# Another order for the last steps of the cross attention and the routing

## The chip, the cores and the metric

The kernel is one program on one core of a Trainium2 chip. Its time is the device time of one execution in microseconds (us), taken over several executions. A separate profiled execution leaves the trace from which the rows below come. Engines are named as the profile names them: PE is the matrix engine, DVE the vector engine, ACT the scalar engine, POOL the engine that scatters rows, SP the queue that issues the plain transfers.

## What is computed

The reference is one decoder layer on 8 sequences of 112 tokens and 512 features (896 tokens, 7 tiles of 128), in fp32:

```python
x = _layernorm(x + _L0_attn_ref(x, W_Q, W_K, W_V, W_O))              # 16 heads, causal
x = _layernorm(x + _L0_xattn_ref(x, ctx_2048, Wq, Wg, bg, Wkv, Wo))  # 375 context rows per sequence
x = _layernorm(x + _L0_ffn_ref(x, router_weight, router_bias, ...))  # 8 experts, the best 2 of each token

# _L0_xattn_ref, cut
kv_summary = jnp.einsum('bhsd,bhse->bhde', k, v)    # k, q through a feature map
z = 1.0 / (jnp.einsum('bhld,bhd->bhl', q, k_sum)[..., None] + EPS)
attn = jnp.einsum('bhld,bhde->bhle', q, kv_summary) * z
out = attn * gate @ Wo.T

# _L0_ffn_ref, cut
logits = h @ router_weight.T + router_bias
top_vals, top_idx = jax.lax.top_k(logits, TOP_K)
...
expert_out = jnp.einsum('eti,eih->eth', act, down_proj) + down_proj_bias[:, None, :]
out = jnp.einsum('te,eth->th', scores, expert_out)
```

## The kernel before

Every engine runs a list of steps that is written out by hand, and waits on semaphores. Large products are split in two parts of the operands and take three passes, so a 128x512 result over 512 features is 12 matmuls (helper `products`, L275). The program goes through the causal attention (two heads at a time), then the linear cross attention, then the routing and the eight experts.

The place of the change is the end of the cross attention and the whole of the late routing. The context of a sequence b is three chunks of 125 rows, so there are 24 chunks n. On PE a chunk is `ctx_k(n)` and `ctx_v(n)`, 12 matmuls each, and `sums(n)`, which adds it to the summary of its sequence in banks 4 and 5. `sums_out(b)` on DVE (L1329) moves the finished summary out, and `attended(b)` on PE (L659) multiplies the queries of sequence b with it. DVE's `attended(b)` divides, `turn_atn(b)` on PE (L668) transposes, and `gated(b)` on DVE (L1393), `a_high(b)` on ACT and `a_low(b)` on DVE make the two parts of the product's input. `cross_out(n)` on PE (12 matmuls, L275 with w_xo) is the output product of token tile n; tile n needs the sequences that it touches, and tiles 5 and 6 need sequences up to 6 and 7.

A token tile then goes through a chain. `cross_add(n)` on DVE adds and takes the statistics, POOL's `inverse_std` makes the inverse deviation, `x2_norm(n)` on DVE (L1350) writes the normalised `row`. `turn_x2(n)` on PE (L686) transposes it, `x2_copy(n)` on ACT (L1026) takes it out of its bank, `router(n)` on PE (L693) makes 8 logits, and `choose(n)` on DVE picks two experts (`chosen`, L1435). `rank(n)` on PE (L703, L704) counts the places in the experts' lists, `assign(n)` on DVE makes the slots (`slot_u`, L1462), and `scatter(n)` on POOL (L425) sends the rows to the experts' lists in HBM. After the last scatter SP fetches the rows of the first three experts (`rows_in`, L352).

Beside it `turn_score(n)` and `down_bias(n)` on PE (L716, L723) make the sum of the experts' output biases of a tile, with `score_copy(n)` on ACT between them; `bias_add(n)` on DVE (L1467) adds it to the row, and `base_store(n)` on SP (L333) writes that to the accumulator in HBM.

The lists are in `block` functions, one for each engine. `CHUNKS` says which chunks run in which iteration of a loop over sequences: four, four, four, three and two; chunk 23 comes behind the loop. Which of the eight PSUM banks a result takes is the place of its step in `late_order` (banks 0 to 3) or `route_order` (banks 6 and 7 by turns); PE waits until the bank's last use has been read. PE enters the expert stage by `gather(0, k)` (L854), the transposes of the fetched rows in banks 4 and 5, and then `gate_up_part` for expert 0 (L275 with w_gu).

Of the kernel before, what the change touches and what calls it, by code (L numbers as in the profile page):

```python
# [23 lines left out]
def decoder_layer(nc: bass.Bass, t: dict, out: bass.AP):  # L24
# [17 lines left out]
    CHUNKS = ((6, 7, 8, 9), (10, 11, 12, 13), (14, 15, 16, 17), (18, 19, 20), (21, 22))  # L42
    DUMP = 3 * P

    with ExitStack() as ctx:
# [175 lines left out]
        def late_order():  # L221
# [13 lines left out]
            rest += [("num", 10), ("num", 11), ("ck", 23), ("turn", 5), ("cv", 23), ("num", 12), ("num", 13), ("wo", 4),  # L235
                     ("turn", 6), ("wo", 5), ("num", 14), ("num", 15), ("turn", 7), ("wo", 6)]
# [3 lines left out]
        def route_order():  # L240
            steps = []
            for n in range(4):
                steps += [("t1", n), ("rt", n), ("rk", n)]
            steps += [("st", 0), ("db", 0), ("t1", 4), ("st", 1), ("db", 1), ("rt", 4), ("t1", 5), ("rt", 5), ("rk", 4),
                      ("rk", 5), ("t1", 6), ("st", 2), ("db", 2), ("rt", 6), ("st", 3), ("db", 3), ("rk", 6), ("cnt", 0)]
            for n in range(4, NT):
                steps += [("st", n), ("db", n)]
            for i, (what, n) in enumerate(steps):
                yield what, n, 6 + i % 2

# [32 lines left out]
        def _(sp):  # L283
# [62 lines left out]
            base_store(0)  # L346
            base_store(1)
# [14 lines left out]
            for n in range(2, NT):  # L362
                base_store(n)
# [41 lines left out]
        def _(pool):  # L405
# [25 lines left out]
            for n in range(4):  # L431
# [62 lines left out]
        def _(pe):  # L494
            late, route = late_order(), route_order()

            def take(of, what, n):
                assert next(of)[:2] == (what, n), (what, n)
                k, turn = place[what, n]
                if turn > 1:  # L500
                    pe.wait_ge(free[k], turn - 1)
                return banks[k]
# [311 lines left out]
            router(3)  # L814
            attended(5)
            sums(22)
            rank(3)
            ctx_k(23)
            turn_atn(5)
            ctx_v(23)  # L820
            attended(6)
            cross_out(4)
            turn_atn(6)
# [12 lines left out]
            rank(4)  # L836
            cross_out(6)
            rank(5)
            turn_x2(6)
            turn_score(2)  # L840
            down_bias(2)
            router(6)
            turn_score(3)
            down_bias(3)
            rank(6)
            count()
            for n in range(4, NT):
                turn_score(n)
                down_bias(n)
# [47 lines left out]
            for k in range(4):  # L897
# [37 lines left out]
        def _(act):  # L935
# [172 lines left out]
            top_tanh(3)  # L1108
# [12 lines left out]
            feature_k(23)  # L1121
            a_high(5)
            score_copy(0)
            a_high(6)
            x2_copy(4)
            score_copy(1)
            top_tanh(4)
            a_high(7)
            x2_copy(5)
            gu_high(0, 0, 0)  # L1130
            top_tanh(5)
            gu_high(0, 0, 1)
            score_copy(2)
            x2_copy(6)
            score_copy(3)
            top_tanh(6)
            gu_high(0, 0, 2)
            gu_high(0, 0, 3)
            for n in range(4, NT):
# [83 lines left out]
        def _(dve):  # L1223
# [386 lines left out]
            choose(3)  # L1610
            attended(5)
            assign(3)
            phi(23)
            gated(5)
            a_low(5)
            v_copy(23)
            attended(6)
            cross_add(4)
            gated(6)
            a_low(6)  # L1620
            sums_out(7)
            x2_norm(4)
            cross_add(5)
            attended(7)
            bias_add(0)
# [175 lines left out]
```

## Time and profile before

| what | us |
|---|---|
| median of 3 runs | 939.78 |
| lowest and highest | 939.7, 941.78 |
| the profiled execution's own time | 941.92 |
| its span, first to last instruction | 940.1 |
| PE busy in the span | 851.5 |
| DVE, ACT, POOL busy | 468.1, 307.7, 100.5 |

All times below are counted from the start of the span. The cross attention's loop runs up to about 640, the routing's last steps from there to 707, and the first expert's products start at 711.04. A row of the timeline gives start, duration, engine, line, operation, result and operands, count, and in square brackets the idle time before it with what ended it. Starts of neighbouring PE rows are up to 0.3 us closer than their durations say, since matmuls overlap and their ends are modelled.

### The profile page before, as it was taken

To read this page: it belongs to the slowest core of one execution; us is meant where nothing else is said; L and a number is where in the kernel's file an instruction comes from. 1 tells how busy PE (TensorE), PEld (TensorE's weight loads), DVE (VectorE), ACT (ScalarE), POOL (GpSimd) and SP (SyncE) were. 2 spreads that over 40 slices of the span, in tenths; PEclk is the share of its full clock that TensorE was granted. 3 is DMA by queue.
4 is the path that set the end of the run, shared out by engine and by line. 5 is a ranking of instruction groups with operands and counts; after the bars stand their busy time and mean duration, and the time that the engine had idled before them with its cause. 6 is when DMAs were issued, how large, how long until landed. Compare 5 with 4: busy or idle time off the path is not lost.

```text
span 940.1 us, 12579 instructions
## 1 busy us (share of the span) xinstructions
PE 851.5 (91%) x4967; PEld 745.8 (79%) x4967; DVE 468.1 (50%) x853; ACT 307.7 (33%) x666; POOL 100.5 (11%) x95
## 2 busy tenths in 40 slices
PE   6999999999999999699999999989769699999990
PEld 5998999999898989578898777778538687877760
DVE  3435454544545352838622443444553666666634
ACT  4443333332314132422442211121212444455430
POOL 0000000000000000000000010101021133333343
PEclk9999999999999999989999999999757799999995
DMA  9940817250202020013100111102455266655225
GB/s 324 353 140 1 260 45 237 69 180 1 90 1 90 1 101 12 1 45 124 33 1 1 33 45 45 56 23 69 156 182 144 107 185 185 185 160 160 70 32 178
DMA packets 34461, 96.99 MB, mean 103 GB/s; under 512 B 5720, under 2 KB 7768, under 8 KB 31712
## 3 DMA queue, kind: packets, MB, share of 16 engines
q1 hardware_dynamic: 30592, 87.70, 27.2%
q0 software_dynamic: 3808, 8.46, 4.6%
q8 instruction: 41, 0.67, 0.3%
q14 instruction: 20, 0.16, 0.1%
HBM read 64.03 MB, written 32.12 MB: 102 GB/s over the span
## 4 chain that ended last, share of the span: by engine, by line
PE 79%; DVE 9%; ACT 5%; issue 5%; DMA 1%; SPq 0%; POOLq 0%; POOL 0%; DVEq 0%; ACTq 0%
PE bank L275 65%; PE bank L589 3%; PE bank L536 2%; PE bank L621 2%; ACT w_gu L937 2%; PE bank L579 1%; PE bank L723 1%; ACT x_g L1145 1%; DVE prob L1263 1%; DVE hh L1687 1%; PE bank L693 1%; PE bank L512 1%; DVE ln_st L1339 1%; DVE up L1678 1%; PE bank L659 1%
## 5 line engine op out<-in xcount | busy, mean ns | idle before, releaser
L275 PE MATMUL bank<-w_kv,cT 128*125 128x512 f32 x576 | 147.5, 407 | 6.5 <-DVE cT L1225 6.5
L275 PE MATMUL bank<-xT,w_qkv 128*128 128x448 f32 x672 | 137.7, 365 | 0.0
L275 PEld LDWEIGHTS bank<-xT,w_qkv 128*128 128x128 f32 x672 | 126.1, 188 | 10.6 <-ACT qT L958 0.4
L275 PEld LDWEIGHTS bank<-w_kv,cT 128*125 128x125 f32 x576 | 106.4, 190 | 31.2 <-DVE cT L1225 6.9
L275 PE MATMUL bank<-x_g,w_gu 128*128 128x288 f32 x768 | 111.0, 303 | 10.1 <-DVE w_gu L1225 9.3
L275 PEld LDWEIGHTS bank<-x_g,w_gu 128*128 128x128 f32 x768 | 107.2, 194 | 11.2 <-DVE w_gu L1225 9.4
L275 PE MATMUL bank<-w_qkv,xT 128*112 128x256 f32 x672 | 85.3, 283 | 0.0
L275 PE MATMUL bank<-w_dn,hT 128*128 128x512 f32 (+1 forms) x288 | 69.9, 397 | 12.4 <-ACT y L1164 10.3
L275 PE MATMUL bank<-w_o,zT 128*128 128x512 f32 x336 | 79.6, 394 | 0.5 <-DVE acc L1540 0.5
L275 PEld LDWEIGHTS bank<-w_qkv,xT 128*112 128x112 f32 x672 | 79.9, 175 | 0.0
L415 POOL TENSOR_TENSOR ln_rs<-ln_ve,half 128x1 f32<-128x1 f32 (+2 forms) x16 | 12.7, 794 | 593.8 <-DVE ln_ve L1345 593.8
L275 PEld LDWEIGHTS bank<-w_o,zT 128*128 128x128 f32 x336 | 61.8, 188 | 14.8 <-DVE acc L1252 1.8
L275 PEld LDWEIGHTS bank<-w_dn,hT 128*128 128x128 f32 (+1 forms) x288 | 45.4, 161 | 33.7 <-ACT y L1164 12.9
L1225 DVE TENSOR_TENSOR w_qkv<-raw_w,w_qkv 128x1024 fp32r<-128x1024 f32 x21 | 25.7, 1225 | 62.4 <-ACT w_qkv L937 62.4
L967 ACT ACTIVATE prob<-prob,neg_max 112x112 f32<-112x112 f32 x128 | 47.7, 374 | 24.3 <-DVE neg_max L1267 24.3
L994 ACT ACTIVATE relu_c<-bank 125x512 f32<-125x512 f32 x24 | 14.3, 598 | 125.1 <-PE bank L275 125.1
L977 ACT CAST zT<-bank 128x448 fp32r<-128x448 f32 x32 | 17.1, 533 | 98.9 <-PE bank L589 98.9
L1311 DVE SCALAR_TENSOR_TENSOR phi_k<-exp_c,relu_c 125x512 f32<-125x512 f32 x24 | 16.6, 692 | 63.4 <-ACT exp_c L995 63.4
L1241 DVE COPY V<-bank 112x512 f32<-112x512 f32 x32 | 22.1, 692 | 51.2 <-PE bank L275 51.2
L463 POOL DMA_INDIRECT y_acc<-y,meta x24 | 41.4, 1724 | 50.0 <-ACT y L1164 45.9
L1252 DVE TENSOR_TENSOR acc<-acc,bank 128x512 f32<-128x512 f32 x49 | 33.6, 687 | 26.1 <-PE bank L275 26.1
L1225 DVE TENSOR_TENSOR w_gu<-raw_gu,w_gu 128x1024 fp32r<-128x1024 f32 x32 | 39.0, 1225 | 8.5 <-ACT w_gu L937 8.5
(144 smaller groups left out, 1169.3 us busy)
## 6 DMA issues: line engine op xcount, KB each, us to landing
x_rows<-blank SPq DMA_DIRECT2D x9, 2084.0 KB, 19.3
raw_gu<-in_w_gu_dram SPq DMA_DIRECT2D x8, 2048.0 KB, 7.8
raw_w<-in_w_qkv_dram SPq DMA_DIRECT2D x21, 512.0 KB, 6.8
raw_dn<-in_w_down_dram SPq DMA_DIRECT2D x8, 1024.0 KB, 8.3
raw_c<-in_ctx_t_dram SPq DMA_DIRECT2D x8, 750.0 KB, 4.4
raw_o<-in_w_o_dram SPq DMA_DIRECT2D x8, 512.0 KB, 3.7
xg<-x_rows SPq DMA_DIRECT2D x8, 512.0 KB, 6.9
raw_kv<-in_w_kv_dram SPq DMA_DIRECT2D x2, 1024.0 KB, 7.0
```

The lines of the kernel that those rows point to most:

```text
L275: last = nc.tensor.matmul(mm_out, lhs(a, k), rhs(b, k), start=(k == 0 and i == 0), stop=(k == n - 1 and i == 2))
L463: nc.gpsimd.indirect_dma_start(y_acc, bass.IndirectOffsetOnAxis(ap=number(k, rows).bitcast(U32), axis=0), y[0:rows, slot(k), :], None, bou ...
L536: mm = nc.tensor.matmul(banks[j][:, 0:HALF], w_first[:, part, a, k, h * E:(h + 1) * E], xT[:, b, k, hf * HALF:(hf + 1) * HALF], start=(k = ...
L589: mm = nc.tensor.matmul(banks[6 + g % 2][:, j * S:(j + 1) * S], V[0:S, p % 2, hf * BH + j, h * E:(h + 1) * E], probT[0:S, g % 2, j, :], st ...
L621: mm = nc.tensor.matmul(banks[4 + g // 2][:, (g % 2) * G1:(g % 2 + 1) * G1], phi_k[0:CM, n % 3, g * P:(g + 1) * P], v_c[0:CM, n % 3, g, :] ...
L937: return nc.scalar.copy(dst, src)
L967: e = nc.scalar.activation(prob[0:S, g, j, :], prob[0:S, g, j, :], ACT.Exp, bias=neg_max[0:S, i:i + 1], scale=-1.0, accum_out=exp_sum[0:S, ...
L977: nc.scalar.copy(zT[:, 0, h, hf * HALF:(hf + 1) * HALF], banks[6 + g % 2][:, 0:HALF])\
L1225: return nc.vector.tensor_tensor(dst, src, bits(hi), ALU.subtract)
L1241: nc.vector.tensor_copy(V[0:S, p % 2, 2 * j:2 * j + 2, :], banks[(1 + j) % 2][0:S, :].rearrange("p (a c) -> p a c", a=2))\
L1252: nc.vector.tensor_tensor(acc[:, n, :], acc[:, n, :], banks[n % 2][:, :], ALU.add)\
L1311: nc.vector.scalar_tensor_tensor(phi_k[0:CM, n % 3, :], exp_c[0:CM, n % 2, :], 1.0, relu_c[0:CM, n % 2, :], ALU.min, ALU.add).then_inc(m[" ...
```

## The change

It is an order change; every engine executes the same computation as before.

- The last three chunks 21, 22 and 23 go one to each of the iterations of sequences 4, 5 and 6, and the token tile's steps are one iteration later than in the loop before.
- The eighth sequence's steps (attended, turn_atn, gated) and cross_out(5), cross_out(6) come ahead of the routing steps of tiles 5 and 6. turn_x2 and router of both tiles stand together, ahead of rank(5) and of the score transposes.
- From turn_score(0) on, the routing's results go round banks 6, 4, 5, 7. The first use of 4 or 5 waits until the summaries have left them (`sum_out`).
- Only bias product 0 stays ahead of rank(6); 1 to 6 stand behind it. PE's gather waits for banks 0 to 5 ahead of its first transpose.
- POOL takes inverse_std(4) ahead of scatter(3), and inverse_std(6) ahead of scatter(4).
- SP issues all seven base stores behind the fetch of the rows; two of them stood ahead of the second expert's weights.

```diff
-    CHUNKS = ((6, 7, 8, 9), (10, 11, 12, 13), (14, 15, 16, 17), (18, 19, 20), (21, 22))
+    CHUNKS = ((6, 7, 8, 9), (10, 11, 12, 13), (14, 15, 16, 17), (18, 19, 20))
...
             for i, (what, n) in enumerate(steps):
                 yield what, n, 6 + i % 2
+            last = [("st", 0), ("rk", 4), ("db", 0), ("t1", 5), ("rt", 5), ("t1", 6), ("rt", 6),
+                     ("rk", 5), ("st", 1), ("rk", 6), ("cnt", 0), ("db", 1)]
+            for n in range(2, NT):
+                last += [("st", n), ("db", n)]
+            for i, (what, n) in enumerate(last):
+                yield what, n, (6, 4, 5, 7)[i % 4]
...
             sp.dma_start(raw_dn[1], t["w_down"][1]).then_inc(in_dn[1], 16)
-            base_store(0)
-            base_store(1)
             sp.wait_ge(*ready("wo", NT - 1))
...
-            for n in range(2, NT):
+            for n in range(NT):
                 base_store(n)
...
-            for n in range(4):
+            for n in range(3):
                 inverse_std(1, n, n + 1, n + 3)
                 scatter(n)
+            inverse_std(1, 3, 4, 6)
             inverse_std(1, 4, 5, 7)
+            scatter(3)
             inverse_std(1, 5, 6, 8)
+            inverse_std(1, 6, 7, 9)
             scatter(4)
-            inverse_std(1, 6, 7, 9)
             scatter(5)
             scatter(6)
...
+                elif k in (4, 5):
+                    pe.wait_ge(m["sum_out"], 2 * NB)
...
+            for b in range(4, 7):
+                n = b + 17
+                attended(b)
+                sums(n - 1)
+                ctx_k(n)
+                turn_atn(b)
+                if b > 4:
+                    turn_x2(b - 2)
+                ctx_v(n)
+                if b > 4:
+                    router(b - 2)
+                if b < 6:
+                    cross_out(b - 1)
+                if b == 5:
+                    rank(3)
             sums(23)
             turn_score(0)
+            attended(7)
             cross_out(5)
-            attended(7)
+            turn_atn(7)
+            rank(4)
             down_bias(0)
-            turn_x2(4)
-            turn_score(1)
-            down_bias(1)
-            router(4)
-            turn_atn(7)
+            cross_out(6)
             turn_x2(5)
             router(5)
-            rank(4)
-            cross_out(6)
+            turn_x2(6)
+            router(6)
             rank(5)
-            turn_x2(6)
-            turn_score(2)
-            down_bias(2)
-            router(6)
-            turn_score(3)
-            down_bias(3)
+            turn_score(1)
             rank(6)
             count()
-            for n in range(4, NT):
+            down_bias(1)
+            for n in range(2, NT):
                 turn_score(n)
                 down_bias(n)
...
-            for k in range(4):
+            for k in range(6):
                 pe.wait_ge(free[k], LAST[k])
```

The lists of ACT and DVE are rewritten in the same order. DVE's new one behind the three iterations:

```diff
             sums_out(7)
-            x2_norm(4)
-            cross_add(5)
+            choose(4)
             attended(7)
...
+            cross_add(5)
+            assign(4)
+            x2_norm(5)
+            cross_add(6)
+            bias_add(0)
+            x2_norm(6)
             choose(5)
+            choose(6)
+            assign(5)
+            assign(6)
             gu_low(0, 0, 0)
...
-            for n in range(4, NT):
+            for n in range(1, NT):
                 bias_add(n)
+                if n in (2, 3):
+                    gu_low(0, 0, n)
```

PE in the kernel before, from cross_out(3) (w_xo) through the last chunk but one, where both chunks of an iteration stand between two attended steps (kv_ext):

```order
L275 MATMUL bank1<-w_xo_83,xT_50 128x512 x12
L275 MATMUL bank2<-w_kv_73,cT1_60 125x512 x12
L621 MATMUL bank4<-v_c_76,phi_k_75 128x132 x2
L621 MATMUL bank5<-v_c_76,phi_k_75 128x132 x2
L275 MATMUL bank3<-w_kv_73,cT1_60 125x512 x12
L686 MATMUL bank7<-ident,row_94 128x128 x4
L693 MATMUL bank6<-rt_w,x2T_95 128x8 x4
L659 MATMUL bank0<-kv_ext2_88,phi_q_85 112x132 x2
```

The same place in the changed kernel:

```order
L278 MATMUL bank1<-w_xo_83,xT_50 128x512 x12
L664 MATMUL bank2<-kv_ext2_88,phi_q_85 112x132 x2
L664 MATMUL bank3<-kv_ext2_88,phi_q_85 112x132 x2
L626 MATMUL bank4<-v_c_76,phi_k_75 128x132 x2
L626 MATMUL bank5<-v_c_76,phi_k_75 128x132 x2
L278 MATMUL bank0<-w_kv_73,cT1_60 125x512 x12
L673 MATMUL bank1<-ident,atn_92 128x112 x4
L691 MATMUL bank7<-ident,row_94 128x128 x4
L278 MATMUL bank2<-w_kv_73,cT1_60 125x512 x12
L698 MATMUL bank6<-rt_w,x2T_95 128x8 x4
L278 MATMUL bank3<-w_xo_83,xT_50 128x512 x12
```

attended(5) has moved ahead of chunk 22, and each transpose or router product now has a chunk's product or an output product behind it.

PE in the kernel before, from the fifth output product (w_xo) to the sixth, with the routing of tiles 4 and 5 between them:

```order
L275 MATMUL bank1<-w_xo_83,xT_50 128x512 x12
L659 MATMUL bank2<-kv_ext1_87,phi_q_85 112x132 x2
L723 MATMUL bank7<-dn_b_96,scoreT_97 128x512
L686 MATMUL bank6<-ident,row_94 128x128 x4
L716 MATMUL bank7<-ident,row_94 8x128
L723 MATMUL bank6<-dn_b_96,scoreT_97 128x512
L693 MATMUL bank7<-rt_w,x2T_95 128x8 x4
L668 MATMUL bank0<-ident,atn_92 128x112 x4
L686 MATMUL bank6<-ident,row_94 128x128 x4
L693 MATMUL bank7<-rt_w,x2T_95 128x8 x4
L703 MATMUL bank6<-chosen,before 128x8
L275 MATMUL bank1<-w_xo_83,xT_50 128x512 x12
```

The same in the changed kernel, and on to the router product of tile 6:

```order
L278 MATMUL bank3<-w_xo_83,xT_50 128x512 x12
L673 MATMUL bank0<-ident,atn_92 128x112 x4
L708 MATMUL bank4<-chosen,before 128x8
L709 MATMUL bank4<-csum,all_ones 128x8
L728 MATMUL bank5<-dn_b_96,scoreT_97 128x512
L278 MATMUL bank1<-w_xo_83,xT_50 128x512 x12
L691 MATMUL bank7<-ident,row_94 128x128 x4
L698 MATMUL bank6<-rt_w,x2T_95 128x8 x4
L691 MATMUL bank4<-ident,row_94 128x128 x4
L698 MATMUL bank5<-rt_w,x2T_95 128x8 x4
```

Between the two output products stand four steps where there were ten, and no transpose of a normalised row is among them.

PE in the changed kernel from rank(6) on; behind the count, six bias products (dn_b) stand ahead of the gather, three in the kernel before:

```order
L709 MATMUL bank4<-csum,all_ones 128x8
L715 MATMUL bank5<-csum,all_ones 128x8
L728 MATMUL bank7<-dn_b_96,scoreT_97 128x512
L721 MATMUL bank6<-ident,row_94 8x128
L728 MATMUL bank4<-dn_b_96,scoreT_97 128x512
L721 MATMUL bank5<-ident,row_94 8x128
L728 MATMUL bank7<-dn_b_96,scoreT_97 128x512
...
L728 MATMUL bank4<-dn_b_96,scoreT_97 128x512
L858 MATMUL bank4<-ident,xg0_106 128x128 x4
```

## Rows read from the trace of the kernel before

**Rows 1.** Windows: busy time by engine; the number before the DMA share is granted clock.

```profile
650.00:660.00 10.00, 8.91 (x52) 7.32 (x50) 5.87 (x14) 1.98 (x5) 2.32 (x3) 1.00 0.68 249
690.00:700.00 10.00, 7.05 (x20) 4.21 (x20) 6.39 (x26) 2.59 (x5) 2.05 (x2) 0.50 0.22 85
```

**Rows 2.** Timeline of PE, the last iterations up to sums(23).

```profile
643.16 0.60 PE L686 MATMUL bank<-ident,row 128*128 128x128 f32 x4
644.43 1.06 PE L693 MATMUL bank<-rt_w,x2T 128*128 128x8 f32 x8 [0.68 <-ACT x2T L1026]
...
654.44 3.06 PE L275 MATMUL bank<-w_xo,xT 128*128 128x512 f32 x12
...
657.72 1.08 PE L621 MATMUL bank<-v_c,phi_k 125*128 125x132 f32 x8
```

**Rows 3.** Timeline of PE, from cross_out(5) to cross_out(6).

```profile
661.21 4.62 PE L275 MATMUL bank<-w_xo,xT 128*128 128x512 f32 x12 [2.30 <-DVE xT L1225]
...
670.29 1.12 PE L723 MATMUL bank<-dn_b,scoreT 8*128 8x512 f32 x2 [0.34 <-ACT scoreT L1036]
...
672.56 0.99 PE L668 MATMUL bank<-ident,atn 112*128 112x112 f32 x4
...
675.87 1.87 PE L693 MATMUL bank<-rt_w,x2T 128*128 128x8 f32 x8 [1.47 <-ACT x2T L1026]
...
678.45 4.72 PE L275 MATMUL bank<-w_xo,xT 128*128 128x512 f32 x12
```

**Rows 4.** Timeline of PE, from turn_x2(6) to the first expert's products.

```profile
686.32 1.11 PE L686 MATMUL bank<-ident,row 128*128 128x128 f32 x4 [2.81 <-DVE row L1350]
...
690.53 1.88 PE L693 MATMUL bank<-rt_w,x2T 128*128 128x8 f32 x8
692.26 0.37 PE L716 MATMUL bank<-ident,row 128*8 128x128 f32 x1
692.98 2.07 PE L723 MATMUL bank<-dn_b,scoreT 8*128 8x512 f32 x2 [0.34 <-ACT scoreT L1036]
694.98 0.60 PE L703 MATMUL bank<-chosen,before 128*128 128x8 f32 x2
...
695.92 0.57 PE L710 MATMUL bank<-csum,all_ones 128*128 128x8 f32 x2
...
707.12 1.97 PE L854 MATMUL bank<-ident,xg 128*128 128x128 f32 x8
...
711.04 8.97 PE L275 MATMUL bank<-x_g,w_gu 128*128 128x288 f32 x48 [0.77 <-DVE x_g L1225]
```

**Rows 5.** Timeline of DVE, steps of the chains in the same stretch.

```profile
661.07 0.77 DVE L1329 TENSOR_TENSOR kv_ext<-bank,blocks 128x264 f32<-128x264 f32 x2
...
674.12 0.62 DVE L1393 SCALAR_TENSOR_TENSOR at<-sig,bank 128x448 f32<-128x448 f32 x1
675.36 0.62 DVE L1225 TENSOR_TENSOR xT<-at,xT 128x448 fp32r<-128x448 f32 x1 [0.63 <-ACT xT L937]
...
693.54 0.17 DVE L1435 TENSOR_TENSOR chosen<-hot 128x8 f32<-128x8 f32 x1
...
695.09 0.69 DVE L1467 TENSOR_TENSOR acc<-row,bank 128x512 f32<-128x512 f32 x1 [1.18 <-PE bank L723]
...
696.67 0.17 DVE L1462 CAST slot_u<-slot_f 128x2 uint32<-128x2 f32 x1
```

**Rows 6.** Timeline of ACT, the copy of tile 6's transposed row.

```profile
687.85 0.57 ACT L1026 COPY x2T<-bank 128x512 f32<-128x512 f32 x1
```

**Rows 7.** Timeline of POOL, scatter(6).

```profile
697.65 1.17 POOL L425 DMA_INDIRECT x_rows<-row,slot_u  x1 [8.04 <-DVE slot_u L1462]
699.12 0.98 POOL L425 DMA_INDIRECT x_rows<-row,slot_u  x1 [0.30 <-issue]
```

**Rows 8.** Timeline of SP's queue: the first fetch of rows, and five base stores.

```profile
702.05 0.38 SPq L352 DMA_DIRECT2D xg<-x_rows  x1
...
710.25 3.75 SPq L333 DMA_DIRECT2D y_acc<-acc  x5
```

More of the change, by code:

```diff
@@ L234, in late_order @@
                     rest += [("wo", b - 1)] * (i == 0 and b > 0)
[L235 to L236 removed]
+            for b in range(4, 7):
+                rest += [("num", 2 * b), ("num", 2 * b + 1), ("ck", b + 17), ("turn", b), ("cv", b + 17)]
+                rest += [("wo", b - 1)] if b < 6 else [("num", 14), ("num", 15), ("wo", 5), ("turn", 7), ("wo", 6)]
             for i, (what, n) in enumerate(rest):
@@ L813, in _ @@
                         rank(b - 1)
[L814 to L823, printed above, removed]
+            for b in range(4, 7):
+                n = b + 17
[12 more added lines that the diff above has]
+                    rank(3)
             sums(23)
             turn_score(0)
+            attended(7)
             cross_out(5)
-            attended(7)
+            turn_atn(7)
+            rank(4)
             down_bias(0)
-            turn_x2(4)
-            turn_score(1)
-            down_bias(1)
-            router(4)
-            turn_atn(7)
+            cross_out(6)
             turn_x2(5)
             router(5)
-            rank(4)
-            cross_out(6)
+            turn_x2(6)
+            router(6)
             rank(5)
-            turn_x2(6)
-            turn_score(2)
-            down_bias(2)
-            router(6)
-            turn_score(3)
-            down_bias(3)
+            turn_score(1)
             rank(6)
             count()
-            for n in range(4, NT):
+            down_bias(1)
+            for n in range(2, NT):
                 turn_score(n)
@@ L1107, in _ @@
                         c_high(n // CT + 1)
-            top_tanh(3)
+            for b in range(4, 7):
+                feature_k(b + 17)
+                a_high(b)
+                if b > 4:
+                    x2_copy(b - 2)
+                    top_tanh(b - 2)
             def use(c):
@@ L1609, in _ @@
                         c_low(n // CT + 1)
[L1610 to L1620, printed above, removed]
+            for b in range(4, 7):
+                attended(b)
+                if b == 4:
+                    sums_out(6)
+                else:
+                    x2_norm(b - 2)
+                phi(b + 17)
+                gated(b)
+                a_low(b)
+                v_copy(b + 17)
+                if b == 5:
+                    choose(3)
+                if b < 6:
+                    cross_add(b - 1)
+                if b == 5:
+                    assign(3)
             sums_out(7)
-            x2_norm(4)
-            cross_add(5)
+            choose(4)
             attended(7)
-            bias_add(0)
-            x2_norm(5)
-            bias_add(1)
-            choose(4)
             gated(7)
             a_low(7)
+            cross_add(5)
[4 more added lines that the diff above has]
+            x2_norm(6)
             choose(5)
-            assign(4)
+            choose(6)
+            assign(5)
+            assign(6)
             gu_low(0, 0, 0)
-            cross_add(6)
-            assign(5)
-            x2_norm(6)
             gu_low(0, 0, 1)
-            bias_add(2)
-            choose(6)
-            bias_add(3)
-            assign(6)
-            gu_low(0, 0, 2)
-            gu_low(0, 0, 3)
             dve.wait_ge(*ready("cnt", 0))
```

23 lines of the change are left out of this document (6 added, 17 removed).

## The prediction, made before the changed kernel was run

> **What bounds the kernel now.** I read the shares of busy time first, then PE's timeline with the idle time ahead of each row, and last the timelines of the engines that those gaps name. PE is busy for most of the span; up to 655 it has hardly a gap and runs at a granted clock of 1.00, the 2.4 GHz level [rows 1]. In the routing's last steps that ends. Between sums(23) at 657.72 [rows 2] and the first expert's products at 711.04 [rows 4], PE waits for DVE's a_low (2.30), for ACT's x2T (1.47), for DVE's row (2.81) [rows 3, 4], and does much of its work at a granted clock of 0.50, the 1.2 GHz level [rows 1]. An output product takes 4.62 and 4.72 there [rows 3], 3.06 at full clock [rows 2]. So this stretch of 53 us is a chain of short steps over four engines in one strict order, and the change is worth what it shortens that chain. Everything behind 711.04 (229.1 us of the span) waits on the start of the expert stage and keeps its order.
>
> At the end of the stretch two things meet. PE finishes the last bias product and goes without a gap to the gather at 707.12 [rows 4]; the rows that it gathers were asked for at 702.05 [rows 8], so they had landed within 5.07. Both paths must be walked for the changed order.
>
> **The change part by part.** I walk the new lists with durations from the rows, wherever an engine takes a step when its operands and the engine are there. All numbers are on the span's clock of before, since nothing ahead of 636 moves.
>
> *Step 1, the three iterations.* PE gets the same work up to sums(23), and in addition turn_x2(4) and router(4), which stood behind it: 0.35 + 0.84 from start to next start (durations 0.60 and 1.06, which overlap the next) [rows 2]. Out goes the wait for x2T ahead of router(3), 0.68 and the overlap lost with it, 0.9 in all [rows 2], since a chunk's product now runs between transpose and router. Sums(23) starts at 657.72 + 1.19 - 0.9 = **658.0**. The wait for a_low hides too: gated, the high and the low part take from 674.12 to 675.98, 1.86 [rows 5], and a product of 12 matmuls of about 3 us stands beside them. If that cover is short in an iteration it costs a piece of 1.86, three times at most; none to 2 us, and I take none, since the cover is longer than the chain.
>
> *Step 2, from sums(23) to cross_out(6).* A new wait comes in: attended(7) now stands directly behind sums(23), so PE waits for sums_out(7) on DVE, 0.04 + 0.77 [rows 5]; behind it in PE's queue stands all the rest. Sums ends at 659.05, attended(7) starts at 659.9, takes 0.85, cross_out(5) 2.87 at full clock (3.06 less the overlap) [rows 2], turn_atn(7) 0.3. That ends at 664.1. DVE, ACT and DVE take 1.9 for gated, high and low [rows 5], covered in part by rank(4) and down_bias(0), about 1.4 at full clock, by their rows at half [rows 3, 4]. So cross_out(6) starts at **666.1** and ends at **669.2**. Before it started at 678.45 and ended at 683.17 [rows 3]. The 14.0 us that this is earlier come from three things: turn_x2, turn_score, down_bias and router steps that now stand earlier or later (6.3), gaps of 2.30, 1.47 [rows 3] and a shorter one against 0.9 and 0.8 (3.3), and half-clock steps at full clock (4.4, the two output products alone 1.6 + 1.7 [rows 2, 3]).
>
> *Step 3, from cross_out(6) to rank(6).* This is one serial chain. From the end of the product to turn_x2(6) it was 683.17 to 686.32, 3.15, by DVE's add and statistics, POOL's power and DVE's row [rows 3, 4]; it stays. Then transpose 1.11, copy 0.57 [rows 6], router 1.88 [rows 4], DVE's choice from 692.41 to the end of chosen at 693.71, 1.30 [rows 4, 5], and 0.04 for each hand-over. In the kernel before, turn_score(2), down_bias(2) stand ahead of router(6), and turn_score(3), down_bias(3) ahead of rank(6), so that it took 11.81 from the product's end to rank(6) at 694.98. Now nothing long is between: 3.15 + 1.11 + 0.57 + 1.88 + 1.30 + 4 x 0.04 = 8.2, and rank(6) starts at **677.3**. That is 17.6 earlier.
>
> *Step 4, from rank(6) to the gather.* Here the change adds to PE. Rank and count take from 694.98 to about 696.35, 1.37 (the count starts at 695.92 [rows 4]). Then six bias products where three stood. Four banks take away the wait of each for the release of the one before it. What stays, as PE's order is score transpose, product, score transpose, is the way over ACT's copy: 0.72 from a transpose's start to the product's, and 2.00 from the product's start to the next, at half clock [rows 4]. So 677.3 + 1.37 + 2.00 + 5 x 2.72 = 694.3; bias_add(6) takes 0.69 [rows 5] and the gather in bank 4 waits for it, new too: **695.1**. It was 12.1 us behind rank(6) and is now 17.8.
>
> The rows' path beside it: DVE has assign(6) done 1.86 behind the start of rank(6) (694.98 to 696.84) [rows 4, 5], so at 679.2. But chosen 5 and 6 come shortly after each other, and assign(5) ends only at about 678.2. POOL starts scatter(5) 0.81 later [rows 5, 7], at 679.0, and one scatter takes 2.45 (697.65 to 700.10) [rows 7]. Scatter(6) is queued behind it and leaves at 681.4 to 683.9. The last row lands and SP issues 1.95 later, at 685.9 [rows 7, 8], and the fetch takes at most 5.07: **690.9**. The rows would be there 4.2 us before PE. The second expert's weights (asked for behind cross_out(6), now about 669) come too long before their use to matter, and two more base stores at the five's rate (3.75 for five, 0.75 each [rows 8]) hold nothing that PE waits for: the accumulator is added to an expert later.
>
> *Step 5, from the gather on.* 707.12 to 711.04 was 3.92 [rows 4]; so the first expert's products start at 699.0 against 711.04, **12.0 us earlier**. What follows has the same order. The first 48 matmuls took 8.97 [rows 4], starting at half clock. If the clock comes back earlier or later there by the length of one output product, that is its surcharge of 1.7 (4.72 - 3.06) either way; I take zero.
>
> *The sum.* -17.6 (steps 1 to 3) + 5.7 (step 4, 17.8 against 12.1) = -12.0 (rounded). The profiled execution took 941.92 for a span of 940.1; with the sum it is 929.9. The median of the runs, 939.78, is 2.1 below the profiled execution, so it goes to **927.8**.
>
> **The rivals.**
>
> *Full clock in the bias products.* In the kernel before, PE did these at 0.50 [rows 1, 4]. The new series has shorter gaps and could bring the clock back. A pair then costs at most 0.72 + 1.12 [rows 3], and the six end at 677.3 + 1 + 1.1 + 5 x 1.84 = 688.6, so that the rows bind at 690.9 and the gain is 16.2: 923.6. The Trainium skill, "TensorE: Matmul & The Clock Gate", Part 1, speaks for this rival: it has the throttled clock as the default state, which activity releases. By that rule a denser series would get the full clock and the time would be near this rival's. Rows 1 speak against it: from 690 to 700, with these same steps on PE, the granted clock stayed at 0.50. I give 0.2.
>
> *The half clock is met earlier.* The gap ahead of attended(7) and the one ahead of cross_out(6) are small, but in the kernel before the clock fell in this very place, behind a gap of 2.30 [rows 3]. If both output products, attended, turn_atn, rank and down_bias run at half clock as in rows 3, steps 2 and 3 take 1.6 + 1.7 + about 1.5 longer: a gain of 7.2, 932.6. I give 0.15.
>
> *The rows bind.* Scatter(4), now behind inverse_std(6), meets the 2 MB of the second expert's weights; if scatters or the fetch take longer by 7 us than above (the issue of one scatter is 2.45, so this means a queue), the gather is at 698 and the gain 9: 930.8. I give 0.1.
>
> *Slower than before.* The three rewritten iterations are full of hand-overs with short covers. If one is missed in each, as with a_low's 2.30 [rows 3], PE could fall to the half clock from 641 on. Then seven products of 12 matmuls (two chunk pairs and three output products) cost 1.65 more each (4.72 against 3.06 [rows 2, 3]), 11.6; the small steps cost some 2.5 more. With the gaps kept that is 14.1 against a gain of 12.0: 2.1 slower, 941.9. It decides only when all seven are at half clock. Against it: 650 to 660 ran at 1.00 with such gaps [rows 1]. I give 0.04.
>
> *No change.* The chain might be as long because DVE, which now does more steps between cross_add(6) and the logits, is the late one. From rows 5 its steps are small. I give 0.01.
>
> **How the numbers follow.** The forecast has 0.5, full clock 0.2, half clock earlier 0.15, the rows 0.1, slower 0.04, no change 0.01. From 923 to 933 the range takes in the first four, with the 1.7 of the clock at the first expert on the forecast and most of the side cases; about 0.15 is left out. A measurement of this kernel can tell some 0.3% (2.8 us) from no change. All but the last two cases are faster by more: 0.94, 0.02 within, 0.04 slower.
>
> **What would show it.** In the changed kernel's PE timeline: sums(23) near 658.0; a wait of 0.8 to 0.9 for L1329's counterpart ahead of attended(7); cross_out(6) ending near 669.2 with about 3.06, not 4.72; rank(6) near 677.3; six bias products 2.7 apart; the gather near 695.1 behind DVE's acc, not behind the fetch; the expert stage near 699.0, and from there to the end 229 us. If the gather waits for the transfer instead, step 4 is wrong; if an output product takes over 4, step 2; if PE shows gaps of over 1 us between 636 and 657, step 1. A different length of the stage behind the gather would mean that the change reaches further than the walk.

## The result, and the profile after

| what | before | after |
|---|---|---|
| median of the runs (4 each; one of before is added to the three above), us | 939.88 | 930.28 |
| lowest and highest | 939.7, 941.78 | 929.8, 930.52 |
| the profiled execution's time | 941.92 | 930.52 |
| its span | 940.1 | 928.7 |
| sums(23) starts | 657.72 | 657.95 |
| cross_out(6) starts | 678.45 | 666.26 |
| rank(6) starts | 694.98 | 676.19 |
| the gather starts | 707.12 | 694.43 |
| first expert's products start | 711.04 | 698.32 |

The changed kernel takes 0.9887 of the time before, 95% interval 0.9872 to 0.9903: 9.6 us faster by the medians, against a forecast of 12.0 and within its range. The expert stage starts 12.7 us earlier (12.0 was forecast). Of that, 11.4 is left in the profiled span and 9.6 in the medians; where the rest goes stands in the part on the prediction.

PE's timeline of the changed kernel from sums(23) on, to be held against [rows 2 to 4]: start, duration, engine, line, operation, result and operands, count, and the idle time before with its releaser.

```profile
657.95 1.14 PE L626 MATMUL bank<-v_c,phi_k 125*128 125x132 f32 x8
658.93 0.27 PE L721 MATMUL bank<-ident,row 128*8 128x128 f32 x1
660.00 1.13 PE L664 MATMUL bank<-kv_ext,phi_q 128*112 128x132 f32 x8 [0.80 <-issue]
660.88 3.03 PE L278 MATMUL bank<-w_xo,xT 128*128 128x512 f32 x12
...
666.26 3.06 PE L278 MATMUL bank<-w_xo,xT 128*128 128x512 f32 x12 [0.56 <-DVE xT L1227]
669.24 0.66 PE L691 MATMUL bank<-ident,row 128*128 128x128 f32 x4
...
672.45 0.66 PE L691 MATMUL bank<-ident,row 128*128 128x128 f32 x4 [0.82 <-DVE row L1352]
673.78 1.06 PE L698 MATMUL bank<-rt_w,x2T 128*128 128x8 f32 x8 [0.68 <-ACT x2T L1030]
...
676.19 0.59 PE L708 MATMUL bank<-chosen,before 128*128 128x8 f32 x2 [0.57 <-DVE chosen L1437]
...
677.56 2.07 PE L728 MATMUL bank<-dn_b,scoreT 8*128 8x512 f32 x2
...
691.17 2.07 PE L728 MATMUL bank<-dn_b,scoreT 8*128 8x512 f32 x2 [0.34 <-ACT scoreT L1040]
694.43 1.94 PE L858 MATMUL bank<-ident,xg 128*128 128x128 f32 x8 [1.19 <-DVE acc L1469]
...
698.32 8.43 PE L278 MATMUL bank<-x_g,w_gu 128*128 128x288 f32 x48 [0.77 <-DVE x_g L1227]
```

The wait of 2.30 ahead of cross_out(5) is gone. That of 2.81 ahead of turn_x2(6) is now 0.82; the chain there isn't shorter (3.13 from the end of cross_out(6) to turn_x2(6), 3.15 before), but PE does tile 5's transpose and router in it. Both output products run at full clock (3.03, 3.06 against 4.62, 4.72 in [rows 3]). The new wait of 0.80 stands ahead of attended(7). The profile names no releaser for it ("issue"), but DVE is moving the summary out just then:

```profile
659.13 0.77 DVE L1331 TENSOR_TENSOR kv_ext<-bank,blocks 128x264 f32<-128x264 f32 x2 [1.32 <-PE bank L626]
```

The price stands at the end: six bias products, and the gather is released by DVE's last addition (acc, L1469), not by the rows. SP had asked for those at 685.62:

```profile
685.62 0.38 SPq L353 DMA_DIRECT2D xg<-x_rows  x1
```

Windows of the changed kernel over this stretch, as in [rows 1] (busy time of PE, its weight loads, DVE, ACT, POOL; then granted clock, DMA share, GB/s): the half clock that before held from 690 to 700, and in cross_out(6) at 678, now begins behind 674.

```profile
660.00:670.00 10.00, 9.33 (x46) 6.88 (x46) 7.03 (x28) 2.03 (x5) 0.57 (x1) 1.00 0.88 369
670.00:680.00 10.00, 7.31 (x34) 4.85 (x34) 8.32 (x40) 4.40 (x9) 4.61 (x5) 0.75 0.82 288
680.00:690.00 10.00, 8.68 (x11) 2.23 (x11) 5.92 (x13) 1.00 (x4) 3.11 (x3) 0.50 0.53 180
```

### The profile page after: what moved, and what is told of

Same layout as the page of the kernel before. It is cut to its first block, busy times and chain, and to the rows that moved or that the text cites. A ratio compares the mean times of both kernels' runs of the same rounds, so it can differ in the third digit from the quotient of the medians.

```text
span 928.7 us, 12580 instructions
## 1 busy us (share of the span) xinstructions
PE 849.5 (91%) x4967; PEld 742.5 (80%) x4967; DVE 468.3 (50%) x853; ACT 307.5 (33%) x666; POOL 100.6 (11%) x95
## 4 chain that ended last, share of the span: by engine, by line
PE 79%; DVE 8%; ACT 5%; issue 5%; DMA 1%; POOL 0%; POOLq 0%; SPq 0%; DVEq 0%; ACTq 0%
PE bank L278 65%; PE bank L594 3%; PE bank L626 2%; PE bank L541 2%; ACT w_gu L941 2%; PE bank L728 1%; PE bank L584 1%; ACT x_g L1147 1%; DVE prob L1265 1%; DVE hh L1690 1%; PE bank L517 1%; PE bank L664 1%; DVE up L1681 1%; ACT y L1166 1%; PE bank L698 1%
## 5 line engine op out<-in xcount | busy, mean ns | idle before, releaser
L416 POOL TENSOR_TENSOR ln_rs<-ln_ve,half 128x1 f32<-128x1 f32 (+2 forms) x16 | 12.7, 792 | 603.7 <-DVE ln_ve L1347 603.7
L278 PEld LDWEIGHTS bank<-w_dn,hT 128*128 128x128 f32 (+1 forms) x288 | 46.6, 165 | 34.1 <-ACT y L1166 12.9
L998 ACT ACTIVATE relu_c<-bank 125x512 f32<-125x512 f32 x24 | 14.3, 598 | 129.8 <-PE bank L278 129.8
```

What stands on the lines that cost most here:

```text
L278: last = nc.tensor.matmul(mm_out, lhs(a, k), rhs(b, k), start=(k == 0 and i == 0), stop=(k == n - 1 and i == 2))
```

## The experiments

Executions differ by a few us in their whole time, so the profiles are compared by two stretches: A, from the start of sums(23) to the start of the first expert's products, and B, from there to the end of the last expert's products. Both are differences of starts and ends in PE's timeline. The runs came in three groups, each with its own runs of the kernel before: median 940.98 for the first four kernels below "changed" in the table, 940.32 for the next four, 941.45 for the last two. Medians of different groups are therefore best compared by their ratios. No run moves the base stores or POOL's steps by themselves; with the base stores in their old place (iterations only) PE's wait ahead of the second expert was 9.27, as in the changed kernel.

| kernel | A | B | median us | ratio to before, 95% interval |
|---|---|---|---|---|
| before | 53.3 | 206.2 | 939.88 | |
| changed | 40.4 | 208.4 | 930.28 | 0.9887 (0.9872 to 0.9903) |
| iterations only | 46.2 | 205.8 | 935.55 | 0.995 (0.993 to 0.9971) |
| tail only | 49.0 | 206.6 | 937.30 | 0.9962 (0.9948 to 0.9976) |
| changed, two banks | 44.2 | 208.2 | 934.72 | 0.991 (0.9877 to 0.9943) |
| changed, pipelined | 39.7 | 206.0 | 929.14 | 0.9872 (0.985 to 0.9894) |
| changed, bias products of four tiles left out | 35.8 | 205.8 | 923.99 | 0.9821 (0.9797 to 0.9844) |
| changed, second expert's weights early | 40.4 | 201.0 | 924.12 | 0.9829 (0.9802 to 0.9855) |
| both | 40.4 | 200.4 | 923.16 | 0.9811 (0.9786 to 0.9835) |
| both, and rank(5) earlier | 41.3 | 203.9 | 925.59 | 0.9832 (0.9805 to 0.986) |
| changed, again | 40.4 | 208.1 | 931.31 | 0.9892 (0.9869 to 0.9915) |
| both, two bias products in gaps | 36.8 | 201.1 | 919.69 | 0.978 (0.9752 to 0.9808) |

### Which part carries the gain

*Iterations only*: the kernel before with the new loop for chunks 21 to 23 and the old order behind sums(23). Its edit on PE (the other engines' lists follow):

```diff
+            for b in range(4, 7):
+                n = b + 17
+                attended(b)
+                sums(n - 1)
+                ctx_k(n)
+                turn_atn(b)
...
             sums(23)
             turn_score(0)
             cross_out(5)
             attended(7)
             down_bias(0)
-            turn_x2(4)
             turn_score(1)
             down_bias(1)
-            router(4)
             turn_atn(7)
```

> The kernel before with one part of the change: chunks 21 to 23 one to each of three iterations, the token tiles' steps one iteration later; everything behind sums(23) keeps the old order, two banks, base stores where they were. Theory (the gain is made by every part of the walk, and the largest is that PE has no old routing steps and no long gaps between sums(23) and cross_out(6)): cross_out(5) starts near 659.1 without a wait for a_low, cross_out(6) near 669 and, if the clock holds, ends near 672 (683.17 before, 669.2 in the changed kernel); from there the old chain of 11.8 and the old 12.1 to the gather: about 696, expert stage near 700, 11 us earlier than before, a time of 929 to 932. Rival (the new order behind sums(23) carries the gain, the iterations only hide two gaps of 0.7 and 2.3): 936 to 938.

Stretch A fell from 53.3 to 46.2, 7.1 of the 12.9 that the whole change takes out of it; the median is 5.4 below its own runs of before. The time of 929 to 932 was missed: 935.55 is just below the rival's 936 to 938. The first half came as expected, cross_out(5) without a wait at 659.31, but the old order then has a wait of its own that the walk of this kernel had overlooked:

```profile
659.31 3.04 PE L276 MATMUL bank<-w_xo,xT 128*128 128x512 f32 x12
...
666.19 1.09 PE L726 MATMUL bank<-dn_b,scoreT 8*128 8x512 f32 x2 [1.69 <-DVE acc L1473]
...
669.68 1.88 PE L696 MATMUL bank<-rt_w,x2T 128*128 128x8 f32 x8 [1.42 <-ACT x2T L1032]
...
672.26 4.37 PE L276 MATMUL bank<-w_xo,xT 128*128 128x512 f32 x12
```

With two banks, down_bias(1) waits for DVE's bias_add(0) (1.69), which stands behind cross_add(5) and attended(7); then the clock halves, and cross_out(6) starts at 672.26, not 669, and takes 4.37. The last products of this profile took 8.59.

*Tail only*: the changed kernel with the old loop.

```diff
-    CHUNKS = ((6, 7, 8, 9), (10, 11, 12, 13), (14, 15, 16, 17), (18, 19, 20))
+    CHUNKS = ((6, 7, 8, 9), (10, 11, 12, 13), (14, 15, 16, 17), (18, 19, 20), (21, 22))
...
             turn_atn(7)
-            rank(4)
+            turn_x2(4)
+            router(4)
             down_bias(0)
             cross_out(6)
+            rank(4)
```

> The changed kernel with the old loop: chunks 21 and 22 in one iteration and 23 behind it, as in the kernel before; the new order only behind sums(23), with transpose and router of tile 4 between cross_out(5) and cross_out(6). Theory: a_low(6) comes at about 661.2 as before, sums_out(7) behind it, so attended(7) starts near 661.9, cross_out(6) near 668.2 and ends at 671.1 at full clock or 674.5 at half; rank(6) 8.2 later and the gather 17.1 behind that: 697 to 700, a time of 932 to 936. Rival (the iterations carry the gain): 937 or more.

A is 49.0, 4.3 less than before. The time, 937.30, missed its 932 to 936 and lies where the rival (937 or more) had it, though the rival is no better for it: the new order behind sums(23) does gain 3.7 in the median. Cross_out(6) was expected near 668.2 and started at 669.86, in a profile in which sums(23) stood 1.6 earlier than in that of before; so it came 3.3 late.

Neither part is the whole: 7.1 and 4.3 add to 11.4 of 12.9 in A. The medians (5.4 and 3.7, together 9.1, against 9.6) can't tell such a remainder from nothing, so it rests on single profiles. In the tail-only profile attended(7) waits for the summary, which DVE moves out behind cross_add(4) and a_low(6); it takes 2.07 where the changed kernel has 1.13, and both output products behind it take longer (3.58 and 4.60 for 3.03 and 3.06). In the changed kernel the three iterations keep this wait at 0.80:

```profile
659.48 0.76 DVE L1327 TENSOR_TENSOR kv_ext<-bank,blocks 128x264 f32<-128x264 f32 x2
660.34 2.07 PE L663 MATMUL bank<-kv_ext,phi_q 128*112 128x132 f32 x8 [3.03 <-issue]
662.06 3.58 PE L277 MATMUL bank<-w_xo,xT 128*128 128x512 f32 x12
...
669.86 4.60 PE L277 MATMUL bank<-w_xo,xT 128*128 128x512 f32 x12
```

*Two banks*: the changed kernel with `6 + i % 2` for the routing's last results.

```diff
-                yield what, n, (6, 4, 5, 7)[i % 4]
+                yield what, n, 6 + i % 2
```

> The changed kernel with the routing's last results in banks 6 and 7 by turns, as before, in place of 6, 4, 5, 7. Theory: router(5) waits for bias_add(0), the second score transpose behind rank(6) for the count's read (near 680.3), and each bias product for the bias_add before it (about 2.9 apart in place of 2.72), so the gather comes 2 to 3 us later: 932 to 933. Rival (the bank round is not needed, PE's pace is set by ACT's copy alone): within 0.5 us of the changed kernel's 930.3.

A is 3.9 longer, where 2 to 3 were expected. By the profile the rival (banks not needed) falls: the waits are the ones named, and behind the first of them router(5) takes 1.84, not 1.06. The times say it less clearly: one of the four executions took 929.25, no more than the changed kernel, and the intervals of the two ratios overlap.

```profile
673.72 1.84 PE L698 MATMUL bank<-rt_w,x2T 128*128 128x8 f32 x8 [2.06 <-DVE acc L1469]
...
685.09 0.37 PE L721 MATMUL bank<-ident,row 128*8 128x128 f32 x1 [0.89 <-DVE most L1646]
686.39 2.04 PE L728 MATMUL bank<-dn_b,scoreT 8*128 8x512 f32 x2 [0.93 <-DVE acc L1469]
...
689.31 2.04 PE L728 MATMUL bank<-dn_b,scoreT 8*128 8x512 f32 x2 [0.56 <-DVE acc L1469]
```

The products are 2.92 apart (686.39 to 689.31), against 2.72 with four banks.

### What ends last ahead of the gather

*Pipelined*: score transpose n+1 ahead of bias product n.

```diff
             count()
-            down_bias(1)
             for n in range(2, NT):
                 turn_score(n)
-                down_bias(n)
+                down_bias(n - 1)
+            down_bias(NT - 1)
```

> The changed kernel with score transpose n+1 ahead of bias product n, so that ACT's copy of 0.72 from transpose to product is hidden behind a product. Theory (PE's bias products end last ahead of the gather, the fetched rows have been there): a pair costs 2.25 at half clock in place of 2.72, the gather comes 2.3 us earlier, 692.1, and the time is 928.0. If PE gets its full clock back by it, the gather is at the rows' landing, at most 690.7, and the time 926.5. Rival (the rows or their landing bind): no change, 930.3.

From rank(6) to the gather it took 16.3 (677.95 to 694.22), against 18.2: the products stand 2.3 apart. The mechanism holds. But the gather came at 694.22, not 692.1: 1.3 of the gain went on a half clock that began at turn_x2(6) already (1.11 for 0.66, router 1.88 for 1.06), so A is only 0.7 shorter, and the median 1.1 below the changed kernel's is no more than the two intervals allow; of the expected 2.3 the time shows no sure part. PE did not get its full clock back, though it was busy for 9.57 of 10 us:

```profile
680.00:690.00 10.00, 9.57 (x13) 2.37 (x13) 7.74 (x14) 1.04 (x5) 3.50 (x4) 0.50 0.55 192
```

*Four left out*: to see when the rows themselves are there. The bias sums of tiles 3 to 6 are left out, so the result is not the layer's.

```diff
             down_bias(1)
-            for n in range(2, NT):
-                turn_score(n)
-                down_bias(n)
+            turn_score(2)
+            down_bias(2)
```

> The changed kernel without the score transposes, bias products and bias additions of token tiles 3 to 6 (left out; those tiles' rows in the accumulator lack the layer's input and the experts' biases). It shows when the rows themselves are there. Theory: in the changed kernel PE's bias products end last ahead of the gather, about 18.2 us behind rank(6); with two of the six left, the gather waits for the fetched rows, which were asked for at 685.6 and land 4.4 to 5.4 later: 690 to 691, 14 to 15 us behind rank(6), 3.5 us earlier than in the changed kernel, a time of 926 to 927. Rival (the rows bind already): gather at 694.4 and 930.

Now the gather is released by the transfer, 13.7 behind rank(6) and 4.36 behind SP's request at 686.32. PE's timeline:

```profile
677.01 0.59 PE L707 MATMUL bank<-chosen,before 128*128 128x8 f32 x2 [0.27 <-DVE chosen L1434]
...
690.68 1.94 PE L856 MATMUL bank<-ident,xg 128*128 128x128 f32 x8 [7.50 <-DMA xg<-x_rows]
```

SP's request stands 9.3 behind rank(6) here and 9.4 in the changed kernel, so in that one too the rows were ready about 18.2 - 13.7 = 4.5 us before PE was. The prediction's step 4 had 4.2. The time, 924.0, is 2 to 3 below what was expected of it; B accounts for that, being 2.6 shorter than in the changed kernel.

### What the expert stage could give

*Second expert's weights early*: ACT's casts and DVE's subtractions for the second expert stand in the time in which the rows travel.

```diff
             for n in range(2, NT):
                 score_copy(n)
+                if n >= 3:
+                    gu_high(1, 1, n - 3)
...
                 if n in (2, 3):
                     gu_low(0, 0, n)
+                if n in (4, 5):
+                    gu_low(1, 1, n - 4)
...
             for k in range(3):
                 gather_low(0, k)
+            gu_low(1, 1, 2)
+            gu_low(1, 1, 3)
```

> The changed kernel with the split of the second expert's gate and up weights moved from between the first expert's steps to the time in which the rows travel: ACT's four casts behind the last score copies, DVE's four subtractions between the last bias additions and behind the first gather. Theory (the 9.27 us that PE waits for w_gu at 723.6 are DVE and ACT doing these splits in line with the first expert's steps, not the transfer): the wait shrinks to 2 us or so, what remains is the hidden part and the gathered rows, and the clock does not fall in it: 7 to 9 us less, 921 to 923. Rival (the transfer of the weights or the chain of the hidden part ends last anyway): 928 or more. If the splits delay bias_add(6) or the first gather, the expert stage starts later by up to 1.2 each.

PE's wait ahead of the second expert fell from 9.27 (released by w_gu, in the changed kernel) to 4.28, which is DVE and ACT finishing the hidden part and the last gathered rows in line:

```profile
718.69 0.26 ACT L1149 CAST x_g<-bank 128x128 fp32r<-128x128 f32 x1
...
719.19 0.28 DVE L1231 TENSOR_TENSOR x_g<-bank,x_g 128x128 fp32r<-128x128 f32 x1
719.58 8.49 PE L278 MATMUL bank<-x_g,w_gu 128*128 128x288 f32 x48 [4.28 <-issue]
```

It is 5.0 us, not 7 to 9; A did not grow. B is 7.4 shorter; the other 2.4 are two groups of matmuls that were slower in the changed kernel's profile (9.31 for 8.49 and 10.17 for 8.60, see below). The median, 924.12, is 6.2 below the changed kernel's and misses its 921 to 923.

*Both* takes this and the pipelined order together; *both, and rank(5) earlier* moves rank(5) ahead of router(6) and assign(5) ahead of choose(6).

> The second expert's weights split early (as in the run ahead of this) together with score transpose n+1 ahead of bias product n. Theory: both act in different places, so the gains add: 2.0 us from the 2.3 us spacing (from rank(6) to the gather it was 16.3 against 18.2 with the pipelined order alone) and 7 to 9 from the splits: 919 to 921. Rival (DVE, which does bias additions and splits in the same stretch, binds): less than either's sum by 1 to 3 us.

> As the run ahead of this, and rank(5) ahead of router(6) on PE with assign(5) ahead of choose(6) on DVE, so that scatter(5) no longer holds up scatter(6) on POOL. Theory (with the bias products at 2.3 apart, PE still ends last, 0 to 2 us behind the rows): scatter(6) leaves 1.5 to 2 us earlier, rank(6) comes 0.5 later, and the time is within 1 us of the run ahead of this. Rival (the rows are what the gather waits for by now): 1.5 us faster.

The two kernels were measured at 923.16 and 925.59. The first misses its 919 to 921: cross_out(6) ran partly at half clock (4.29 for 3.06) in its profile, and A, 40.4, is no shorter there than without the pipelined order; the median is 1.0 lower. In the second the request for the rows did go out earlier, at 685.81 against 687.90, but rank(6) waited 1.15 for chosen and PE's bias products ended the stretch at the same place (694.79 against 694.84). So rows that come earlier gain nothing while PE ends last. Its time is 2.4 above the first's, outside what was expected; the profile shows B 3.5 longer, with the expert stage in the same order, and three groups of the same matmuls make up all of it (9.33 for 8.20, 9.00 for 8.14, 10.13 for 8.60). Whether the reordering or the clock made the medians differ is not settled.

*Both, two bias products in gaps*: bias products 1 and 2 into PE's two waits for x2T, with results in banks of the cross attention that are free by then.

```diff
+            free_now = {("st", 1): 2, ("db", 1): 3, ("st", 2): 0, ("db", 2): 2}
...
             down_bias(0)
+            turn_score(1)
             cross_out(6)
             turn_x2(5)
+            turn_score(2)
+            down_bias(1)
             router(5)
             turn_x2(6)
+            down_bias(2)
             router(6)
             rank(5)
-            turn_score(1)
             rank(6)
             count()
-            down_bias(1)
...
```

> The second expert's weights split early and the score transposes pipelined, as in the run of both, and bias products 1 and 2 with their transposes moved ahead: their results in banks 0, 2 and 3, which the cross attention has left, the products in PE's waits for x2T (0.68 each). Theory (PE's bias products are what ends last ahead of the gather even with the pipelined order, 694.8 against rows that could be there at 692.3): each product ahead costs 0.4 us of rank(6) and takes 2.3 from the tail, so the gather waits for the rows, near 692, and the time is 2 to 3 us below the run of both (923.2): 920 to 921.5. Rival (rank(6) comes later by as much as the tail gets shorter): 923.

919.69, the fastest of all, 0.978 of before (0.9752 to 0.9808), and 0.3 below the expected range; one of its six executions took 925.37, and its interval just overlaps with that of *both*. The waits of 0.68 ahead of both routers are filled, rank(6) starts 18.6 behind sums(23) (18.2 in the changed kernel), 0.4 later where 0.8 was expected, and the gather, 14.3 behind rank(6), waits for the transfer at last:

```profile
669.60 0.66 PE L698 MATMUL bank<-ident,row 128*128 128x128 f32 x4
670.10 0.27 PE L728 MATMUL bank<-ident,row 128*8 128x128 f32 x1
670.30 1.12 PE L735 MATMUL bank<-dn_b,scoreT 8*128 8x512 f32 x2
671.35 1.06 PE L705 MATMUL bank<-rt_w,x2T 128*128 128x8 f32 x8
...
691.22 1.94 PE L869 MATMUL bank<-ident,xg 128*128 128x128 f32 x8 [2.59 <-DMA xg<-x_rows]
```

### The changed kernel again

> The changed kernel once more, for its own spread and a second profile. Question: the expert stage started 12.7 us earlier in the changed kernel's profile, yet its span is only 11.4 shorter; from 698.3 on, the second expert's first products took 9.31 (8.11 before) and the last expert's 10.17 (8.61 before). Theory (where the half clock begins and ends at these two waits differs from execution to execution, whatever the order): in this profile the two rows fall anew on about 8.0 to 9.3 and on 8.6 or 10.15, the stretch from sums(23) to the first expert's products is again 40 to 42 us, and the median is 929 to 932. Rival (the new order costs 2.7 us in the expert stage): again 9.3 and 10.15, and the same length behind the start.

A is 40.4 once more and the median 931.31, 10.1 below its runs of before (941.45). The two rows fell on 9.24 and 10.14, as in the first profile (9.31, 10.17). So this run alone does not speak against the rival. The other kernels do in part: the pipelined one and the one with four products left out keep the changed kernel's expert stage word for word, and have 8.06 and 7.99, and 8.60 for the last. So it isn't the order within the stage, but they enter it at other times. The last products of the changed and of the pipelined kernel:

```profile
896.55 10.17 PE L278 MATMUL bank<-w_dn,hT 128*128 128x512 f32 x36 [2.19 <-DVE w_dn L1227]
```

```profile
895.53 8.60 PE L279 MATMUL bank<-w_dn,hT 128*128 128x512 f32 x36 [2.19 <-DVE w_dn L1228]
```

Work, operands and the wait of 2.19 are the same; the granted clock in 890 to 900 was 0.84 in the first and 1.00 in the second. In all twelve profiles the two rows go together: where the second expert's first products took 9.0 or more (changed twice, two banks, both with rank(5) earlier), the last took 10.13 to 10.17, elsewhere 8.59 to 8.61. What decides between the two durations stays open, and the rival isn't refuted: no kernel was seen with both durations, and both profiles of the changed kernel have the longer one. Its executions without a profile lean the same way. With the shorter durations its two profiled ones would have taken some 2.7 less, about 928; of its ten executions none took less than 929.39. That isn't proof, since other parts vary too (cross_out(3), ahead of the change, starts anywhere from 632.17 to 635.07 in the twelve profiles).

## Why the prediction was right

It was right in sign, in its range, and in the mechanism of each step up to the gather; the forecast was 2.4 us too far. That it came so near has some luck in it: step 3 was 1.3 too long, and that hid a part of what was lost behind the gather.

- **Step 1** (the iterations). Sums(23) at 658.0; measured 657.95, with no gap over 0.5 ahead of it from 636 on. The stretch ahead of 636 was 0.46 earlier in this execution (cross_out(3) at 633.31 for 633.77), so the step itself cost about 0.7, not 0.3, and 0.46 of the 12.7 at the expert stage isn't the change's.
- **Step 2** (to cross_out(6)). Attended(7) at 659.9, measured 660.00, with the new wait at 0.80; cross_out(6) from 666.1 to 669.2, measured 666.26 to 669.32. The rival with an earlier half clock did not occur in the changed kernel's profiles; in those of *both* and of *both, and rank(5) earlier* cross_out(6) did take 4.29, 1.2 more.
- **Step 3** (to rank(6)). 8.2 from the product's end to rank(6) was expected, 6.9 measured. Transpose and router of tile 6 had the full clock (0.66 and 1.06), where the step had taken the half-clock 1.11 and 1.88: 1.3 too much.
- **Step 4** (to the gather). 17.8 was expected, 18.2 measured, with the products 2.72 apart as forecast and the gather behind DVE's addition (1.19 from the last product's end, not 0.8). The request for the rows was expected at 685.9 and came at 685.62, but that is two errors in turn: rank(6) was 1.1 early, and from there the request took 9.4, not 8.6, because scatter(5) held POOL for 3.3 and not for 2.45. The fetch, put at 5.07 at most, then took 4.4 in the two kernels in which the gather waited for it (4.36 and 4.45). Leaving four products out showed that the rows would have been there 4.5 us before PE (4.2 in the prediction).
- **Full clock in the bias products** (0.2). It did not come: 2.07 each and a granted clock of 0.50, also in the pipelined order with PE busy for 9.57 of 10 us. The Trainium skill, "TensorE: Matmul & The Clock Gate", Part 1, has activity release the throttled clock; here PE's being busy by the profile did not, and the measurement decides.
- **Step 5** (from the gather on). Here is the term that was mis-sized. The first expert's products started 12.7 us earlier, and the profiled span is 11.4 shorter. The prediction took zero for the clock behind the gather, with 1.7 either way, and looked for it at the first expert's products only. The first expert gained 0.54 (8.43 for 8.97), the second lost 1.2 (9.31 for 8.11) and the last 1.56 (10.17 for 8.61): 2.2 together, at two later waits that the prediction had no term for. After the last products 0.9 came back. Whether the new order brings these 2.2 or chance does is open (above).
- **From the profile to the median.** The sum was made against a profiled execution of 941.92, 2.0 above the median of before; that of the changed kernel, 930.52, lies 0.24 above its own. The prediction carried the difference of 2.1 over as if it belonged to every execution. That is the other 1.8 between 11.4 and 9.6. In the runs of the changed kernel again, against their own before, the gain is 10.1.

## What to carry to other kernels

When several engines finish a stage by short steps in turn, write the new order down as a walk with the durations of the old trace, for both the path of the results and the queue of the engine that feeds it: it gave starts within 1.2 us over 40 in the changed kernel. It isn't always so near: in *iterations only* and *tail only* the same walk had cross_out(6) 3.3 us too early, and of the ten expected times only that of the changed kernel again held its median. Work put behind the last result to shorten its path has to fit the time in which that result travels; six products of 2.7 us did not fit 13.7, and the fix was to pipeline their transposes and to fill the short waits ahead with two of them. And where the same instructions can get one clock or the other, look at which of them the profiled execution had before its difference to the median goes into a forecast.

## What was not expected of the hardware

The same 36 matmuls behind the same wait of 2.19 took 8.60 or 10.15 us in the profiles of different kernels, at a granted clock of 1.00 or 0.84 in the 10 us in which they start (pipelined and changed), and this went together with the second expert's first products, 170 us earlier. The Trainium skill, "TensorE: Matmul & The Clock Gate", Part 1, says that the number of slow matmuls at a kernel's start varies from run to run. No run here shows that for one kernel: the two profiles of the changed kernel have 9.31 and 9.24, 10.17 and 10.14. What varies here lies behind waits in mid-kernel, and from kernel to kernel, with 8.0 to 9.3 for the 48 matmuls of the second expert. And the bias products behind rank(6), mostly 2.3 us apart and with PE busy for 9.57 to 9.64 of the 10 us from 680, stayed at 2.04 to 2.07 each and a granted clock of 0.50 in all three kernels that have that order throughout.
